# A perceiver kernel on one core: the first cross attention's stacked keys laid out in two 64-row halves, and its score maxima taken from 64-row matmul pairs

## The reference

```
x = x + xattn(layernorm(x), ctx, ctx, mask, Wq, bq, Wk, bk, Wv, bv, Wo, bo)
qh = (q @ Wq.T + bq)  # 32 x 16 heads x 64 rows x 8
kh = (k @ Wk.T + bk)  # 32 x 16 heads x 1601 keys x 8
attn = softmax(where(valid, qh @ kh.T * scale, -inf)); out = (attn @ vh) @ Wo.T + bo
```

## Time and profile before

| | us |
|---|---|
| median of three runs | 3107.3 |
| the profiled execution | 3106.7 |
| its span | 3105.0 |
| TensorE busy | 2835.4 (91%) |
| VectorE busy | 1989.1 (64%) |
| GpSimd busy | 1905.7 (61%) |
| ScalarE busy | 1480.3 (48%) |

### The profile page before, as it was taken

The page is one execution under the profiler, slowest core; times in us unless marked ns, Lnnn a source line. Parts: engine busy times, 40 slices in busy tenths (PEclk is TensorE's granted clock), DMA queues, the critical chain, the costliest instruction groups (busy, mean ns, idle before and its releaser), DMA issues. The chain is left out here.

```text
span 3105.0 us, 67073 instructions
## 1 busy us (share of the span) xinstructions
PE 2835.4 (91%) x22829; PEld 1630.0 (52%) x22829; DVE 1989.1 (64%) x4520; ACT 1480.3 (48%) x2387; POOL 1905.7 (61%) x1278
## 2 busy tenths in 40 slices
PE   5599999999999978998899999999999997887789
PEld 2355555555555566776344444444444443777356
DVE  5477777777777745114566777766777744776653
ACT  3366666666666522333554454444444434223633
POOL 5387878787878721001478888878888872553500
PEclk8799999999999988998999999999999998999789
DMA  6755555555555201001000000000000000000300
GB/s 175 168 185 182 188 180 191 177 194 174 197 173 187 99 3 56 1 0 38 22 22 32 21 23 30 21 22 31 21 27 26 21 1 9 3 3 11 76 4 10
DMA packets 148251, 233.13 MB, mean 75 GB/s; under 512 B 16787, under 2 KB 85851, under 8 KB 148124
## 3 DMA queue, kind: packets, MB, share of 16 engines
q1 hardware_dynamic: 147836, 231.23, 23.3%
q10 hardware_dynamic: 288, 0.13, 0.0%
HBM read 147.80 MB, written 83.52 MB: 74 GB/s over the span
## 5 line engine op out<-in xcount | busy, mean ns | idle before, releaser
L446 POOL TENSOR_TENSOR sb_a_acc<-sb_a_acc,sb_a_PT 128x1024 f32<-128x1024 f32 x252 | 595.8, 2364 | 44.7 <-ACT sb_a_PT L524 38.3
L608 DVE TENSOR_REDUCE sb_a_mx<-ps_a_A 128x1 f32<-128x512 f32 x768 | 506.5, 686 | 106.0 <-PE ps_a_A L772 100.9
L524 ACT ACTIVATE sb_a_PT<-ps_a_SC 128x1024 f32<-128x1024 f32 (+1 forms) x416 | 425.8, 1024 | 296.8 <-PE ps_a_SC L795 271.6
L1693 POOL TENSOR_TENSOR sb_a_acc<-sb_a_acc,sb_a_PT 128x512 f32<-128x512 f32 (+2 forms) x384 | 487.6, 1270 | 37.2 <-ACT sb_a_PT L1789 10.9
L1789 ACT ACTIVATE sb_a_PT<-ps_a_SC 128x1024 f32<-128x1024 f32 (+2 forms) x256 | 234.3, 916 | 563.0 <-PE ps_a_SC L2068 328.2
L1882 DVE TENSOR_REDUCE sb_a_mx<-ps_a_A 128x1 f32<-128x512 f32 x384 | 256.7, 679 | 280.0 <-PE ps_a_A L2043 280.0
L2087 PE MATMUL ps_a_PV<-sb_a_PT,sb_a_XN 128*128 128x512 f32 (+2 forms) x896 | 434.3, 601 | 0.7 <-ACT sb_a_PT L1789 0.7
L2068 PE MATMUL ps_a_SC<-sb_a_QX,sb_a_XT 128*128 128x512 f32 (+1 forms) x832 | 396.7, 596 | 0.0
L772 PE MATMUL ps_a_A<-sb_a_KS,sb_a_QS 97*128 97x512 bf16 x768 | 301.3, 393 | 13.3 <-DVE sb_a_QS L600 7.1
L795 PE MATMUL ps_a_SC<-sb_a_QS,sb_a_KS 105*128 105x128 bf16 (+1 forms) x3328 | 256.8, 220 | 13.5 <-DVE sb_a_QS L622 13.5
L806 PE MATMUL ps_a_PV<-sb_a_PT,sb_a_V 128*32 128x256 f32 (+1 forms) x3328 | 266.3, 392 | 0.4 <-issue 0.3
(11 more groups left out here) (521 smaller groups left out, 5260.6 us busy)
## 6 DMA issues: line engine op xcount, KB each, us to landing
sb_a_C<-in_ctx_dram SPq DMA_DIRECT2D x64, 768.0 KB
a_KD<-sb_a_K SPq DMA_DIRECT2D x192, 256.0 KB, 4.0
sb_a_KS<-a_KD SPq DMA_DIRECT2D x256, 192.0 KB
a_KD<-sb_a_K SPq DMA_DIRECT2D x192, 144.2 KB, 2.7
sb_a_KS<-a_KD SPq DMA_DIRECT2D x256, 108.2 KB
sb_a_QP<-a_QD SPq DMA_DIRECT2D x6, 384.0 KB, 16.7
sb_a_dn<-n_L_ffn_expert_down_dram SPq DMA_DIRECT2D x1, 2048.0 KB, 15.2
a_QD<-sb_a_PT SPq DMA_DIRECT2D x3, 384.0 KB, 5.7
```

Of the source, the lines that this page charges most:

```text
L446: pool.tensor_tensor(acc[:, :], first[:, :], PT[slot(a, j)][:, :], ALU.add).then_inc(s["acc"], 1)
L524: act.activation(PT[slot(a, j)][0:n, :], SC[(a + j) % 2][0:n, :], ACT.Exp).then_inc(s["exp"], 1)
L608: v.tensor_reduce(mx[:, p, c:c + 1], A[u % 2][:, :], AXX, ALU.max).then_inc(s["am"], 1)
L1693: pool.tensor_tensor(acc[a][0:m, :], first, PT[u % 4][0:m, HQ * i:HQ * i + HQ], ALU.add).then_inc(s["acc"], 1)
```

## The change

The stack gets 128 rows in two halves of 64. For an even pair, rows 0 to 63 are the bias, fifteen rows for the subtraction of the maximum, and the three leading products of pieces; rows 64 to 127 have a constant row, unused rows and the three small products. For an odd pair the halves change places. The maxima are taken from the leading half alone (an approximate maximum; the softmax is the same with any value near it), so an even and an odd pair are two matmuls of 64 rows, on different rows, into the two banks of one PSUM tile AA, and one reduce takes both. There are 13 units instead of 26, placed by `PLACES`. Unit 0 now stands in tile step 0. The unit waits for the reduce of the unit just before it. The scores are over all 128 rows. Five spilled copies instead of six; each read of the stack becomes two of 48 partitions; the bias row is read twice. GpSimd presets KS and QP rows with ones. The first batch's maxima (`tops_apart`) handle the banks one by one.

```diff
-    COUNT = (0, 2, 2, 2, 2, 3, 3, 3, 3, 3, 3, 0, 0)
-    PIECES = (0, 1, 2, 0, 1, 0)
+    LEAD, TAIL = (2, 3, 4), (0, 1, 2)
+    PLACES = {0: (EARLY,), 1: (EARLY,), 2: (EARLY,), 3: (EARLY,), 4: (MIDDLE, LATE), 5: (LATE,), 6: (LATE,), 7: (LATE,),
+              8: (MIDDLE, LATE), 9: (LATE,), 10: (LATE,)}
+    PIECES = (2, 1, 0, 1, 0)
...
-                sp.dma_start(KS[a][ROWM:ROWM + 1, :, lo:hi], k.bias_rows[dsl(b), lo:hi].unsqueeze(1).to_broadcast([1, NP, hi - lo]))\
-                  .then_inc(s[f"kd{a}{g}"], 16)
-                sp.wait_ge(s[f"kw{g}"], 96 * b + 96)
+                for r in (0, 64):
+                    sp.dma_start(KS[a][r:r + 1, :, lo:hi], k.bias_rows[dsl(b), lo:hi].unsqueeze(1).to_broadcast([1, NP, hi - lo]))\
+                      .then_inc(s[f"kd{a}{g}"], 16)
+                sp.wait_ge(s[f"kw{g}"], 80 * b + 80)
                 for w in range(NP):
-                    sp.dma_start(KS[a][0:96, w, lo:hi], KD[a][:, 16 * w:16 * w + 16, lo:hi]).then_inc(s[f"kd{a}{g}"], 16)
+                    for r in (16, 80):
+                        first = (LEAD if half(w).start < r < half(w).stop else TAIL)[0]
+                        sp.dma_start(KS[a][r:r + 48, w, lo:hi], KD[a][first:first + 3, 16 * w:16 * w + 16, lo:hi]).then_inc(s[f"kd{a}{g}"], 16)
...
-                for r, part in enumerate((0, 0, 0, 1, 1, 2)):
-                    sp.dma_start(QP[16 * r:16 * r + 16, :, lo:hi], QD[part][:, lo:hi].rearrange("(w i) s -> i w s", i=16)).then_inc(sem, 16)
+                for r in (1, 5):
+                    sp.dma_start(QP[16 * r:16 * r + 16, :, lo:hi], QD[0][:, lo:hi].rearrange("(w i) s -> i w s", i=16)).then_inc(sem, 16)
+                for o in range(2):
+                    for r, part in zip((4 * o + 2, 4 * o + 3, 6 - 4 * o, 7 - 4 * o), (0, 1, 1, 2)):
+                        src = QD[part][:, lo:hi].rearrange("(w o i) s -> o i w s", o=2, i=16)[o]
+                        sp.dma_start(QP[16 * r:16 * r + 16, o:NP:2, lo:hi], src).then_inc(sem, 16)
...
             for i in range(2):
-                pool.memset(QS[i][96:P, :, :], 0.0).then_inc(s["pz"], 1)
+                pool.memset(KS[i][0:80, :, :].rearrange("p w s -> p (w s)").bitcast(F32), ONE16).then_inc(s["kz"], 1)
...
             def tops(b, u):
-                wait(v, s["as"], NU * b + u + 1)
-                if u < 24:
-                    p, c = u % NP, u // NP
-                    v.tensor_reduce(mx[:, p, c:c + 1], A[u % 2][:, :], AXX, ALU.max).then_inc(s["am"], 1)
+                wait(v, s["as"], FIRST + NU * b + u + 1)
+                if u < 12:
+                    w, c = u % 4, u // 4
+                    v.tensor_reduce(mx[:, 2 * w:2 * w + 2, c], AA[:, :, :], AXX, ALU.max).then_inc(s["am"], 1)
...
+            def ready(b, a, u):
+                if u == 0:
+                    wait(pe, s["qe"], 2 * (b + 1))
+                if u in (0, 8):
+                    pe.wait_ge(s[f"kd{a}{u // 8}"], 144 * (b - a) + 288)
+            def maxima(a, u, o):
+                if u < 12:
+                    p, c = 2 * (u % 4) + o, u // 4
+                    return pe.matmul(A[o], QS[a][half(p), p, :], KS[a][half(p), p, 512 * c:512 * c + 512], start=True, stop=True)
...
+            def tops(b, a, u):
+                ready(b, a, u)
+                wait(pe, s["am"], FIRST + NU * b + u)
+                maxima(a, u, 0)
+                maxima(a, u, 1).then_inc(s["as"], 1)
...
-                    mm = pe.matmul(SC[(a + j) % 2][0:m, P * p:P * p + P], KS[a][0:ROWS, p, P * j:P * j + m], QS[a][0:ROWS, p, :], start=True, stop=True)
+                    mm = pe.matmul(SC[(a + j) % 2][0:m, P * p:P * p + P], KS[a][:, p, P * j:P * j + m], QS[a][:, p, :], start=True, stop=True)
...
+                    us = lambda place: units(j, place) if n1 else ()
+                    for u in us(EARLY):
                         tops(b + 1, 1 - a, u)
                     if j + 1 < NK:
                         scores(b, a, j + 1)
```

More of the change, by code:

```diff
@@ L246, in stage_xattn0 @@
     SP2 = S + 1
-    ROWM, ROWH = 96, 97
-    ROWS = ROWH + NP
-    COUNT = (0, 2, 2, 2, 2, 3, 3, 3, 3, 3, 3, 0, 0)
-    PIECES = (0, 1, 2, 0, 1, 0)
+    LEAD, TAIL = (2, 3, 4), (0, 1, 2)
+    EARLY, MIDDLE, LATE = 0, 1, 2
+    PLACES = {0: (EARLY,), 1: (EARLY,), 2: (EARLY,), 3: (EARLY,), 4: (MIDDLE, LATE), 5: (LATE,), 6: (LATE,), 7: (LATE,),
+              8: (MIDDLE, LATE), 9: (LATE,), 10: (LATE,)}
+    PIECES = (2, 1, 0, 1, 0)
+    ONE16 = 1.0 + 2.0 ** -9 - 2.0 ** -16
     GROUPS = ((0, 1024), (1024, S))
@@ L273, in stage_xattn0 @@
     half2 = sb("half2", [P, 2])
-    NU = 26
+    NU = 13
+    FIRST = 13
     SPANS = ((0, 8 * T), (8 * T, B * T))
@@ L283, in stage_xattn0 @@
     PV = k.ps("a0_PV", [P, 2, G * T], F32, ctx)
-    A = [k.ps(f"a0_A{i}", [P, 512], F32, ctx) for i in range(2)]
+    AA = k.ps("a0_A", [P, 2, 512], F32, ctx)
+    A = [AA[:, i, :] for i in range(2)]
     M = k.ps("a0_M", [P, 512], F32, ctx)
@@ L303, in dsl, with units, half @@
         return bass.ds(b, 1)
-    def units(j):
-        return range(sum(COUNT[:j]), sum(COUNT[:j + 1]))
+    def units(j, place=None):
+        n = sum(len(PLACES.get(i, ())) for i in range(j))
+        return [n + i for i, at in enumerate(PLACES.get(j, ())) if place in (None, at)]
+    def half(p):
+        return slice(64 * (p % 2), 64 * (p % 2) + 64)
     def summed(b):
@@ L389, in _ @@
             pieces(0)
+            sp.wait_ge(s["kz"], 2)
             stack(0, 0, 0)
             sp.wait_ge(s["qw"], 48)
+            sp.wait_ge(s["kz"], 3)
             spread(*SPANS[0], s["ldq0"])
@@ L582, in _ @@
             v.tensor_reduce(half2[:, :], k.heads[:, :].rearrange("p (h i) -> p i h", i=2), AXX, ALU.add).then_inc(s["qe0"], 1)
+            v.wait_ge(s["qe0"], 1)
+            for r in (0, 64):
+                v.memset(half2[r:r + 16, :], 0.0).then_inc(s["qe0"], 1)
+            v.wait_ge(s["qe0"], 3)
+            for r in (0, 64):
+                v.memset(half2[r:r + 1, :], 1.0).then_inc(s["qe0"], 1)
             norm_vector(k, v, s["n"])
@@ L649, in step @@
                     emptied(b - 1)
+                if n1:
+                    for u in units(0):
+                        tops(b + 1, u)
+                if old:
                     final(b - 1)
@@ L823, in step @@
                 for j in range(NK):
-                    us = units(j) if n1 else ()
-                    for u in us[0:1]:
+                    us = lambda place: units(j, place) if n1 else ()
+                    for u in us(EARLY):
                         tops(b + 1, 1 - a, u)
@@ L830, in step @@
                         scores(b + 1, 1 - a, 0)
-                    for u in us[1:2]:
+                    for u in us(MIDDLE):
                         tops(b + 1, 1 - a, u)
@@ L840, in step @@
                         top(b + 1)
-                    for u in us[2:]:
+                    for u in us(LATE):
                         tops(b + 1, 1 - a, u)
@@ L857, in _ @@
                     pe.wait_ge(s["qc"], c - 1)
-                pe.matmul(A[c % 2][:, :], k.w0T["q"], k.hT[:, 512 * c:512 * c + 512], start=True, stop=True).then_inc(s["q"], 1)
+                pe.matmul(A[c % 2], k.w0T["q"], k.hT[:, 512 * c:512 * c + 512], start=True, stop=True).then_inc(s["q"], 1)
             for c in range(4):
```

96 lines of the change are left out of this document (46 added, 50 removed).

## The result

The changed kernel takes 3604.9 us, the median of four runs (3604.0 to 3607.6). The kernel before, run beside it, took 3108.2 us: a ratio of 1.160 [1.159, 1.162], so 497 us more. The forecast was slower, 3544 us, and the range of 3470 to 3630 holds the result.

A forecast was written before the change was run, and what follows sets the result against it. TensorE was taken to bound the kernel before, at 31.0 us a step; halved stack reads would make it 44.7. 29 steps add 397 us, before the loop 40: 437 us on 3106.7 gives 3544 us, range 3470 to 3630.

The forecast's parts named there:

- Three engines, the same three for both halves: Stack reads: each 48-row read runs on the same three DMA engines, at 75 GB/s instead of 150; chance 0.86.
- The step as a sum, 44.7 us: Loop step: waits, transfer and cold clock add up to 44.7 us instead of 31.0, over 29 steps 397 us.
- 19.1 + 0.7 + 1.5 = 21.3 us: Step: 19.1 us from first maxima unit to next stack read, 0.7 extra bias read, 1.5 cold clock.
- 2.1 + 21.0 + 0.4 = 23.5: Step, from first stack read to maxima unit: 2.1 us to full rate, 21.0 transfer of group 0, 0.4 landing.
- The landing: Step: time after group 0's transfer until its data counts as arrived, estimated at 0.4 us.
- 40 us before the loop: Before the loop: slower stack reads of batches 0 and 1 cost 29 us, batch 2's group 0 brings it to 40.
- done before the first third piece at 32.66: nothing: Before the loop: GpSimd's two KS presets, 6.0 us each if elements count, end before its first third piece, costing nothing.
- TensorE's own work counted at 0: TensorE in a step: paired matmuls save at most 2.5 us, shape changes cost 1.5; counted 0 because the DMA wait covers it.
- two waits of 0.5 us: TensorE at tiles 4 and 8: two close units, the second waiting about 0.5 us for the reduce just before.
- The three-and-three engines: Rival, stack reads: the second half uses three other engines, step 32.8 us, 3160 us in all; chance 0.07.
- The rival on the other side, sixteen engines: Stack reads spread over 16 engines, TensorE decides, step 28.5 to 31.0 us, 3025 to 3107 us; chance 0.07.
- The queue that grows on the three engines: Rival: spills queue behind group 1 on the three engines, step 47 to 50 us, 3610 to 3700 us; chance 0.10.

The follow-up runs named there:

- b_half: The kernel before, with only each read of the stack cut into two reads of 48 rows (three pieces each): 3502.2 us.
- a_tile1: The changed kernel with unit 0 of the maxima moved from tile step 0 back to tile step 1: 3524.2 us.
- b_third: The kernel before, with each read of the stack cut into three reads of 32 rows (two pieces each): 4036.2 us.
- a_order: The changed kernel with VectorE doing the final sums of the batch before ahead of the reduce of unit 0, not behind it: 3593.6 us.
- a_wide_order: The changed kernel with both the flat-row DRAM order of a_wide and the VectorE order of a_order: 3114.5 us.
- a_same_rows: a_wide_order with both matmuls of a 512-column unit on rows 0 to 63, so they cannot run side by side: 3172.3 us.
- a_wide: The changed kernel with the DRAM copy of the keys reordered so each 48-row stack read is one flat run of rows: 3212.1 us.
- b_wide: The kernel before with the DRAM copy of the keys reordered so each 96-row stack read is one flat run of rows: 3097.3 us.
- a_best2: a_wide_order with KS presets on ScalarE, QP's preset behind VectorE's normalisation, and tile 4's second unit moved ahead of the scores: 3104.5 us.

## Why the prediction was right

The runs give the parts of the loss: b_half alone 12.2 us a step (43.20 - 31.02), and the unit moved up a tile 2.7 (46.33 - 43.62). The order on VectorE, 0.4 by itself (46.33 - 45.92), is no third part, since a_tile1 removes that collision as well. That makes 14.9 of 15.3; the last 0.4 us, between b_half and a_tile1, was not tried apart (the second bias read, 0.7 us in SP's queue, is a candidate). Before the loop the split costs 41.8 us (216.7 - 174.9), and the rest of the change 10.8 (227.5 - 216.7).

- **Three engines, the same three for both halves.** Shown: a share of 0.19 to 0.21, the step of b_half and the row six, three, two of b_third. The Trainium skill's rule in "DMA: Bandwidth & Descriptors", section on why a DMA increments its semaphore by 16, would have it so; the runs agree at outermost sizes of 6, 3 and 2 (shares of 0.39, 0.19 to 0.21 and 0.13) and of 48 and 96 flat rows, multiples of 16, which ran at up to 0.83 and 1.07.
- **The step as a sum, 44.7 us.** It measured 46.33, and the term that was too small is spread over both parts. From the unit to the next first read I had 19.1 + 0.7 + 1.5 = 21.3 us; the trace has 684.28 - 662.25 = 22.0. From the read to the unit I had 2.1 + 21.0 + 0.4 = 23.5; the trace has 24.3. Of that, 0.5 is the rate: the four windows of 1 us average 73.3 GB/s and not 75, so 1.57 MB take 21.5 us. The landing, put at 0.4 us without a row, is about 0.6 (the group's last completions at 661.6, the unit at 662.25). Of the first part, 0.4 is the collision on VectorE (a_order), which the prediction did not have at all; the remaining 0.3 was not tried apart, but the half clock behind the wait lasts 5 us where the sum took 4. Over 29 steps the term was too small by 29 x 1.6 = 47 us.
- **40 us before the loop.** It measured 52.6. The part for the reads was right (41.8 in b_half). The step that failed is "done before the first third piece at 32.66: nothing" for the presets: the first third piece starts at 38.77. The length was near (10.81 us for the two, 5.4 each against 6.0, so elements count and not bytes), but I asked only what GpSimd itself had behind them, and not which engine beside it they hold up. Taking that away, in the form with wide reads, is worth 7.7 us by the trace and 5.6 by the times. The rest of the 10.8 us (the bias reads, the four more DMAs of the spread) was not tried apart.
- **TensorE's own work counted at 0.** Right, but not only for the reason given, the cover of the long wait. In a_wide_order nothing covers it, and the step is 31.03 us against 31.02: 2.5 us saved (a_same_rows: the pair really runs at once), by the sum 15 x 0.1 = 1.5 us spent on shape changes, and about 1.0 us of waits for the reduce. The size of the last is partly luck: I had two waits of 0.5 us, and there are five of 0.14 to 0.32. The 1.5 us are counted from the spacing of starts and no run takes the changes away by themselves. The reduce of two banks measured 1.22 us, between the ends of 0.69 and 1.38.
- **The rivals.** The three-and-three engines fell with b_half and b_third. The rival on the other side, sixteen engines, was right as to what would happen then: it allowed 31.0 us a step at worst, and a_wide_order has 31.03. But it also took for granted that only TensorE would be the bound; in a_wide it was first the collision, at 34.3. The queue that grows on the three engines did not come: the steps are even, 45.8 to 47.0 us each up to the last two (44.9 and 44.8), and show no holes piling up.

I said what would show me right: share and rate (yes), starts 44.7 us apart (46.33), a wait of some 12 us ended by the stack's read (12.35 us), a granted clock of 0.5 behind it (yes), two maxima matmuls starting together (0.003 to 0.007 us apart), later stages unchanged (0.8 us).

**The version that is best** is the kernel before with the new DRAM order alone, b_wide: 3097.3 us, 0.3% less than before. The change in its best form, a_best2, is 0.16 us a step faster than b_wide but starts the loop 7.2 us later. Why it starts later was not tried apart; it has 16 reads a group where b_wide has 8, and the presets.

## What to carry to other kernels

Before a transfer is cut by partitions, look at what its outermost size is on both sides, and compare that with 16 times its DMA share, taken while it alone is running: a share of 0.39 was six full engines and ten empty ones, and the cut halved the six. The mean of 0.57 over a whole step hid this. A layout in DRAM in which the rows of one read are a single flat run repairs it; the writes into that layout then ran on half of the engines, which cost nothing here.

When engine time is saved by two smaller matmuls at once, subtract the changes of shape (0.1 us each here) and the longer reduce behind them before hoping for the gain; here 2.5 us became nothing.

An edit that is worth nothing beside a long stall can be worth much once the stall is gone (the order on VectorE: 0.4 us a step with it, 3.3 without), so test repairs together, not only one at a time.

## What the runs showed of the hardware that I had not expected

- GpSimd's long operations hold some of VectorE's up until they end. A 128x64 operation of 0.20 us took 1.98 us beside an add of 2.35 us, one of 0.28 took 2.38, and a cast of 0.43 us took 7.28 us beside a memset of 6.92. A memset reads nothing from SBUF and still does it. The reduce of line 636, which reads PSUM, stayed between 1.15 and 1.23 us in all its instructions of the changed kernel.
- A read of flat rows is also issued faster. For the same 192 KB SP took 0.73 us with six pieces of 16 rows and 0.45 us with 96 flat rows (b_wide, 8 in 3.63 us). It took 0.46 us for each wide read of 48 rows (a_wide, 16 in 7.31 us), and 0.83 to 0.90 us for each read of three pieces of 16 rows (13.28 and 14.34 us for 16); how much of the latter is SP held back by three full engines was not tried. At 96 KB each, 0.46 us is 215 GB/s, and the windows of a_wide show 201 to 219: there SP's issue sets the rate, not the 16 engines, whose share is 0.69 to 0.83.
